# Window attention on one core: all score products of a slot in one call, value products in turn through the column groups

## The reference, cut to what matters

```python
qkv = xw @ qkv_w.T + qkv_b
qkv = qkv.reshape(b * nw, N, 3, NH, hd).transpose(2, 0, 3, 1, 4)
q, k, v = (qkv[0] * hd ** (-0.5), qkv[1], qkv[2])
attn = jnp.einsum('bhnd,bhmd->bhnm', q, k)
attn = attn + bias[None]            # and a shift mask
attn = jax.nn.softmax(attn, axis=-1)
out = jnp.einsum('bhnm,bhmd->bhnd', attn, v).transpose(0, 2, 1, 3).reshape(b * nw, N, c)
out = out @ proj_w.T + proj_b
```

## Time and profile before

| | |
|---|---|
| runs | 4394.44 us median (4394.0 to 4397.97) |
| profiled execution | 4384.42 us, span of the trace 4382.6 us |
| attention part | about 2337 to 4377 us, 128 units |
| a unit in the steady state | 15.83 us |
| TensorE's granted clock | full in the attention part |

### The profile page before, as it was taken

The page is one execution under the profiler, slowest core; times in us unless marked ns, Lnnn a source line. Parts: engine busy times, 40 slices in busy tenths (PEclk is TensorE's granted clock), DMA queues, the critical chain, the costliest instruction groups (busy, mean ns, idle before and its releaser), DMA issues. The chain is left out here.

```text
span 4382.6 us, 142449 instructions
## 1 busy us (share of the span) xinstructions
PE 4170.2 (95%) x51550; PEld 3612.2 (82%) x51550; DVE 3617.6 (83%) x8006; ACT 2658.1 (61%) x5150; POOL 3076.1 (70%) x2292
## 2 busy tenths in 40 slices
PE   0699999999999999999997999999999999999999
PEld 0588888888888888888886888888888888888887
DVE  8677777777777777777766999999999999999998
ACT  0355555555555555555554777777777777777776
POOL 0477777777777777777765777777777777777776
PEclk9999999999999999999998999999999999999999
DMA  8011111111111111111112222222222222222222
GB/s 371 23 42 41 41 41 41 41 41 41 41 41 41 41 41 41 41 41 41 41 34 68 76 76 77 77 76 76 76 75 76 76 76 77 76 76 77 78 76 65
DMA packets 390777, 284.67 MB, mean 65 GB/s; under 512 B 148159, under 2 KB 389188, under 8 KB 389700
## 3 DMA queue, kind: packets, MB, share of 16 engines
q1 hardware_dynamic: 387612, 281.57, 22.1%
q10 hardware_dynamic: 3112, 2.39, 0.2%
HBM read 119.00 MB, written 87.31 MB: 47 GB/s over the span
## 5 line engine op out<-in xcount | busy, mean ns | idle before, releaser
L941 POOL TENSOR_TENSOR L<-L,mx 128x588 f32<-128x588 f32 x512 | 600.2, 1172 | 595.5 <-DVE mx L1164 595.4
L634 PE MATMUL ps_o<-w,g_hi 128*128 128x384 f32 x2352 | 722.9, 367 | 5.3 <-DVE g_lo L588 1.9
L437 ACT ACTIVATE gF<-ps_g,b1f 128x512 f32<-128x512 f32 x588 | 404.0, 687 | 395.3 <-PE ps_g L673 362.9
L935 POOL TENSOR_TENSOR E<-E,ri 128x588 f32<-128x588 f32 x512 | 600.3, 1172 | 0.8 <-DVE ri L1170 0.8
L634 PE MATMUL ps_o<-w,g_lo 128*128 128x192 f32 x2352 | 534.1, 254 | 0.0
L1226 PE MATMUL ps_s<-Kp,Q 32*64 32x98 f32 x12288 | 493.5, 258 | 21.9 <-issue 19.4
L1048 ACT ACTIVATE o_hi<-ps_v,vb 128x98 fp32r<-128x98 f32 (+1 forms) x1024 | 289.1, 334 | 301.1 <-PE ps_v L1339 293.6
L634 PEld LDWEIGHTS ps_o<-w,g_hi 128*128 128x128 f32 x2352 | 428.9, 189 | 28.7 <-DVE g_lo L588 26.4
L634 PEld LDWEIGHTS ps_o<-w,g_lo 128*128 128x128 f32 x2352 | 442.7, 190 | 0.0
L1160 DVE SCALAR_TENSOR_TENSOR L<-ps_s,bias 128x588 f32<-128x588 f32 x512 | 394.7, 771 | 54.8 <-PE ps_s L1226 37.5
L491 POOL TENSOR_TENSOR g_lo<-gF,g_hi 128x512 fp32r<-128x512 f32 x196 | 314.2, 1622 | 172.7 <-ACT g_hi L442 172.7
(11 more groups left out here) (240 smaller groups left out, 12553.6 us busy)
## 6 DMA issues: line engine op xcount, KB each, us to landing
xs<-in_x SPq DMA_DIRECT2D x8, 4704.0 KB, 22.5
xt<-in_x SPq DMA_DIRECT2D x98, 384.0 KB, 3.4
xb<-x_cells SPq DMA_DIRECT2D x128, 294.0 KB
Vx<-V SPq DMA_DIRECT2D x512, 73.5 KB
out<-yo SPq DMA_DIRECT2D x128, 294.0 KB
x_cells<-x SPq DMA_DIRECT2D x780, 48.0 KB
Kp<-K SPq DMA_DIRECT2D x256, 98.0 KB, 1.9
Kp<-K SPq DMA_DIRECT2D x256, 49.0 KB, 2.2
```

The source lines that it names most:

```text
L437: act.activation(gF[f % 4][:, :], ps_g[:, f % 2, :], ACT.Gelu, bias=b1f[:, f:f + 1]).then_inc(s_gelu, 1)
L634: last = pe.matmul(dst, g[:, f, P * k:P * (k + 1)], w, start=(f == 0 and i == 0), stop=(f == FT - 1 and i == 1))
L935: pool.tensor_tensor(e, e, ri[p][:, :].unsqueeze(2).to_broadcast([P, HEADS, T]), ALU.mult)\
L941: pool.tensor_tensor(l, l, mx[p][:, :].unsqueeze(2).to_broadcast([P, HEADS, T]), ALU.subtract).then_inc(s_sub, 1)
```

## The change

Pair g moves to row group g % 2, and to chunk 0, 2 or 1 for g // 2 = 0, 1, 2. All pairs of one bank are now in one row group (0 or 1), Q and Kp have 64 partitions and three chunks. All 12 score products go in one call ahead of the transposes, and the second call and its semaphore are gone. The queries' evacuation from 128 partitions becomes two of 64. The keys' spread has six DMAs of 32 rows instead of two of 32 and two of 64. The value products are written in the order `PAIR_TURN` of (window, pair), by column group 0, 1, 2, 3, 0, 1, then 2, 3, 0, 1, 0, 1. Products, transposes and their number stay the same.

```diff
+            PAIR_TURN = ((0, 0), (0, 1), (0, 2), (0, 3), (0, 4), (0, 5), (1, 2), (1, 3), (1, 0), (1, 1), (1, 4), (1, 5))
-            Q = [sb(f"Q{b}", [P, 2, NW, SLOT]) for b in range(2)]
+            Q = [sb(f"Q{b}", [CB, 3, NW, SLOT]) for b in range(2)]
-            Kp = [sb(f"Kp{b}", [P, 2, HB, NW, T]) for b in range(2)]
+            Kp = [sb(f"Kp{b}", [CB, 3, HB, NW, T]) for b in range(2)]
-            K_SPREADS = 2 * HB
+            K_SPREADS = 3 * HB
             def pair_rows(g):
-                return slice(2 * HD * (g % PA), 2 * HD * (g % PA + 1)), g // PA
+                row = 2 * HD * (g % 2)
+                return slice(row, row + 2 * HD), (0, 2, 1)[g // 2]
...
                         sp.wait_ge(s_qkm, 3 * (u + 1) + 1)
-                        for k, count in ((1, CB), (0, P)):
-                            if k == 0:
+                        for k, first, chunk in ((1, 0, 1), (0, 0, 0), (0, CB, 2)):
+                            if chunk == 0:
                                 sp.wait_ge(s_qkm, 3 * (u + 1) + 2)
                             for e in range(HB):
-                                rows = slice(e, count, HB)
-                                sp.dma_start(Kp[d][rows, k, e, :, :], K[rows, k, :, :]).then_inc(s_kp[d], 16)
+                                sp.dma_start(Kp[d][e:CB:HB, chunk, e, :, :], K[first + e:first + CB:HB, k, :, :])\
+                                  .then_inc(s_kp[d], 16)
...
-                        last = act.activation(Q[d][:, 0, :, 0:T], full, ACT.Identity, bias=par[d][:, 2:3])
+                        for chunk, rows in ((0, slice(0, CB)), (2, slice(CB, P))):
+                            last = act.activation(Q[d][:, chunk, :, 0:T], full[rows], ACT.Identity,
+                                                  bias=par[d][rows, 2:3])
...
-                            scores(c, p, (0, 3, 1, 4)).then_inc(s_scx, 1)
+                            scores(c, p, (0, 3, 1, 4, 2, 5)).then_inc(s_sc, 1)
...
-                        if is_unit(u):
-                            pe.wait_ge(s_scx, UP * u + p + 1)
-                            scores(c, p, (2, 5)).then_inc(s_sc, 1)
...
-                            for w in range(2):
-                                for j in range(JP):
-                                    g = PAIR_AT[j]
-                                    row, col = 2 * HD * (g % PA), T2 * (g // PA) + T * w
+                            for w, g in PAIR_TURN:
+                                j, row, col = PAIR_AT.index(g), 2 * HD * (g % PA), T2 * (g // PA) + T * w
```

More of the change, by code:

```diff
@@ L808, in build @@
             s_vx = [sem(f"v_spread{b}") for b in range(2)]
-            s_scx, s_sc, s_lg, s_mx = sem("scores_first_rows_summed"), sem("scores_summed"), sem("logits"), sem("row_maxima")
+            s_sc, s_lg, s_mx = sem("scores_summed"), sem("logits"), sem("row_maxima")
             s_sub = sem("maxima_off")
@@ L991, in queries_b @@
                     upto(act, s_sc, UP * (v - 1))
-                    act.activation(Q[1 - c][0:CB, 1, :, 0:T], full[CB:P], ACT.Identity,
+                    act.activation(Q[1 - c][:, 1, :, 0:T], full[CB:P], ACT.Identity,
                                    bias=par[1 - c][CB:P, 3:4]).then_inc(s_qb, 1)
@@ L1334, in slot @@
                             upto(pe, s_o, k)
-                            for w in range(2):
-                                for j in range(JP):
-                                    g = PAIR_AT[j]
-                                    row, col = 2 * HD * (g % PA), T2 * (g // PA) + T * w
[L1339 to L1342, removed]
+                            for w, g in PAIR_TURN:
+                                j, row, col = PAIR_AT.index(g), 2 * HD * (g % PA), T2 * (g // PA) + T * w
+                                last = pe.matmul(ps_v[row:row + 2 * HD, col:col + T],
+                                                 Vx[lc][0:T2, 2 * lp + w, g:2 * HD * JP:JP],
+                                                 PT[lp % 2][0:T2, j, T * w:T * (w + 1)],
+                                                 start=True, stop=True)
                             last.then_inc(s_pv, 1)
```

## The result

The changed kernel takes 4315.97 us (median of 4 runs, 4312.2 to 4322.27) against 4394.22 us before (4 runs), a ratio of 0.9823 with a 95% interval of 0.9809 to 0.9836: 78 us faster, where 91 were forecast. Its profiled execution took 4312.2 us.

A forecast was written before the change was run, and what follows sets the result against it. TensorE's own chain bounds the kernel, with VectorE near. Gains of 0.20 us a slot, 102 us, less 9 for x_hi and 2 at the start, make 91: 4394.4 to 4303 us, range 4284 to 4335.

The forecast's parts named there:

- Scores in one call: TensorE's score products: one call of 0.67 us replaces pieces of 0.50 and 0.33, net 0.16 us a slot.
- Value products in turn: TensorE's value products in the new order: 0 to 0.08 us a slot to gain, 0.04 taken.
- x_hi late for project(0): PE waits 0.14 us before project(0) for VectorE's x_hi in 64 odd units, 9 us in all.
- VectorE's lap: VectorE's own work per unit, mean 14.98 us, just under PE's new 15.03, or 15.10 with the x_hi wait.
- The first rival: DVE or ACT takes part back: a unit ends near 15.3 to 15.5 us, 4320 to 4360 us; chance 0.18.
- The second rival: Matmul starts are in order, turns halve the value phase, DVE's 14.98 stops the gain: 4285 us; chance 0.03.
- The evacuations of the queries: One more ScalarE activation per unit, 0.58 us at most, in slot 3: costed at nothing, up to 0.3 if cover fails.
- The keys in the steady state: Two more spread issues add 1.15 us to SP; keys still land with slack 0.5 before slot 0: no cost.
- The start: Start of the attention part: Kp's zeroing 0.7 us longer and two more issues, 1.2, in the first unit: 2 us.

The follow-up runs named there:

- the kernels without the wait: Changed kernel with row sums over 25 tokens: 4298.89 us; with slot 0's reciprocal behind x_hi and rs first: 4306.44; plus second query evacuation behind E: 4301.23.

## Why the prediction was right, and where it was mis-sized

**Scores in one call: right.** The pieces are 0.67 and 0.47 as forecast, and the unseen boundary from transposes to middle work costs what transposes to scores did (0.146 between starts).

**Value products in turn: right in size, partly by luck, and not everywhere.** 0.043 a slot against 0.04, which was the middle of a range of 0 to 0.08 and not worked out. The range itself was too wide: it gave the fullest groups' eight matmuls 0.42 us, and they take 0.45. At the loop's turn the new order brings nothing: PE's "issue" before slot 0 is 16.9 us in 46 after, 14.8 in 46 before, 0.05 us in two units.

**x_hi late for project(0): the right place, too small by the matmul behind it.** The term was 0.14 in two units and measured 0.21 (30.39 less the 30.16 to 30.20 of the kernels without the wait). PE's timeline of the changed kernel at `project(0)`, odd unit and then even:

```profile
3009.14 0.25 PE L1280 MATMUL ps_w<-wproj_b_lo,o_hi 128*98 128x192 f32 x1
3009.37 0.45 PE L1252 MATMUL ps_w<-x_hi,wqkv_a_hi 128*128 128x392 f32 x1
3009.66 0.34 PE L1252 MATMUL ps_w<-x_lo,wqkv_a_hi 128*128 128x392 f32 x1
...
3024.63 0.25 PE L1280 MATMUL ps_w<-wproj_b_lo,o_hi 128*98 128x192 f32 x1
3024.72 0.38 PE L1252 MATMUL ps_w<-x_hi,wqkv_a_hi 128*128 128x392 f32 x1
3024.94 0.34 PE L1252 MATMUL ps_w<-x_lo,wqkv_a_hi 128*128 128x392 f32 x1
```

The first matmul comes 0.23 after the one ahead of it instead of 0.09: the 0.14 of the forecast. It is so in every odd unit from 2700 to 4200 us, 0.144 on the mean. The second comes 0.29 after the first instead of 0.22, 0.07 more behind a stop. The same 0.28 stands between the first two matmuls of `project(1)`, which follow the transposes without any wait, so it is not the wait as such that costs it, and its cause stays open. And x_hi ended where it was put: 5.79 after slot 0's scores here, 5.85 on the mean of the odd units, where 5.85 was forecast. So the wait was sized right, and the step that the forecast left out is the matmul behind it (VectorE in the changed kernel):

```profile
3004.34 0.31 DVE L1147 SCALAR_TENSOR_TENSOR o_lo<-ps_v,vb,o_hi 128x98 fp32r<-128x98 f32 x1
...
3008.70 0.62 DVE L1130 SCALAR_TENSOR_TENSOR x_hi<-ps_w,par,x_hi 64x392 fp32r<-64x392 f32 x1
```

**VectorE's lap: near, and not the bound**, as forecast; work taken from it gave only the x_hi wait back, and a mere change of its order gave the same. The first rival, in which VectorE takes part of the gain back, had that much of the truth: the unit is 15.20 where 15.10 were forecast, and 0.035 of that comes with x_hi. The second, starts in order, falls with the products group by group.

**The evacuations of the queries: costed at nothing, rightly** in both kernels; the wait for E appeared and cost nothing. **The keys in the steady state: nothing, rightly**, though the slack hangs on rs.

**The start: 2 us forecast, 3 to 11 measured** for the six spreads alone. The forecast counted issues and zeroing and left the clock out, and the section on the profile before calls the clock full in the attention part, which it is not in all of the first 25 us (0.83 in the window above). The fourth unit's `turn` starts 4.6 us later in the changed kernel's trace than before, but between traces of kernels with the same start that moment moves by several us (2378.7 in the kernel before, 2386.1 with its shorter row sums, where the clock was lower), so the size stays rough.

The sum again with what was measured: two units 31.68 to 30.39, 1.29 x 64 = 83 us, less about 5 at the start, 78. The 5 is what closes the sum; the six spreads alone, 5.2 at the medians, agree with it. The forecast had 1.46 x 64 - 2 = 91. Read place by place, 0.17 are missing in two units: 0.07 are x_hi's, 0.03 the second matmul of `project(0)`, which comes 0.015 later than before in both units, 0.035 the value products with the loop's turn, and 0.03 are spread over the rest.

**Slips in the working.** VectorE's odd lap adds up to 14.95, not 14.91, so its mean was 15.00, only 0.03 under PE's 15.03. The second rival counts 8 steps for the new order; started one by one by its own rule the new list takes 12 steps and the old 16, so it would have gained half of what it says. The first rival's unit of 15.3 to 15.5 is 0.2 to 0.4 above the forecast's, not 0.3 to 0.6. None of the three moves the forecast.

## What to carry to other kernels

Where an engine's own groups set the time, count the boundaries: calls of the same shape put together saved a boundary each, 0.16 us here, and the pieces of the chain gave it to 0.01. When the bound engine gets faster, look for the one handoff that arrives just behind it, and add to the wait what the next matmul loses behind it (0.14 and 0.07 here). Before moving work to a later place on an engine off the path, follow what its queue releases down to the DMAs: here a reciprocal 2 us later became late keys. And read the granted clock at the start of a part, not only in its steady state.

## What was not expected of the hardware

TensorE starts matmuls of another column group ahead of earlier ones, but not without limit: with all of a group's products in line the phase went from 0.51 to 0.79 us, and behind a group of eight the next began when the fifth of them had begun. The first matmul behind a stop of PE was followed 0.07 us later than usual by the next. At the turn of the loop a shorter phase did not bring the next unit's scores earlier (0.61 us instead of 0.54 behind it).
